# Attention scores by two half-arrays of 64 rows, the zero-padded queries removed, TensorE's attention steps written out

## What is computed

```python
q = split_heads(layernorm(x) @ Wq.T + bq) * 16 ** -0.5      # bq in block 1 only
k, v = split_heads(ctx @ Wk.T + bk), split_heads(ctx @ Wv.T + bv)
logits = einsum('bhqd,bhkd->bhqk', q, k) + bias             # block 1: a mask instead
x = x + einsum('bhqk,bhkd->bhqd', softmax(logits), v).reshape(...) @ Wo.T + bo
```

## Time and profile before

| | us |
|---|---|
| median of 3 runs | 956.08 |
| lowest, highest run | 948.71, 956.51 |
| the profiled execution | 949.21 |
| its span, first to last instruction | 947.2 |
| TensorE busy in the span | 776.4 (82%) |
| VectorE busy | 498.9 (53%) |
| GpSimd busy | 422.4 (45%) |
| ScalarE busy | 293.5 (31%) |

### The profile page before, as it was taken

One profiled execution on the slowest core, in us unless ns is written; L12 is line 12 of the kernel. 1 busy time (PEld: TensorE's weight loads), 2 busy tenths in 40 slices (PEclk: granted clock), 3 DMA queues, 4 the chain that ended last, 5 costly groups with the idle time before them and its releaser, 6 DMA issues. The chain is left out here.

```text
span 947.2 us, 16638 instructions
## 1 busy us (share of the span) xinstructions
PE 776.4 (82%) x4409; PEld 619.4 (65%) x4411; DVE 498.9 (53%) x1644; ACT 293.5 (31%) x804; POOL 422.4 (45%) x463
## 2 busy tenths in 40 slices
PE   4799999687994499999985588889497059999995
PEld 3688887344662367777763477667385059999994
DVE  2788886543331465555543699999472113333331
ACT  1455554011221144444432244444241012212220
POOL 1343342033767344554543776667452133443431
PEclk8999998598998599999998699999795579999998
DMA  7333333401200144444463223334556456555540
GB/s 204 132 128 106 98 116 104 113 18 13 25 8 0 33 127 135 141 142 135 138 125 102 70 76 111 112 111 134 67 67 84 84 180 202 175 183 196 189 164 1
DMA packets 62007, 103.05 MB, mean 109 GB/s; under 512 B 22313, under 2 KB 43273, under 8 KB 60556
## 3 DMA queue, kind: packets, MB, share of 16 engines
q1 hardware_dynamic: 48076, 73.08, 27.3%
q0 software_dynamic: 13600, 27.33, 11.5%
q10 hardware_dynamic: 288, 2.10, 0.6%
HBM read 82.77 MB, written 22.44 MB: 111 GB/s over the span
## 5 line engine op out<-in xcount | busy, mean ns | idle before, releaser
L601 POOL DMA_INDIRECT U<-normed,idx x95 | 91.1, 959 | 97.8 <-DVE idx L1123 79.7
L586 POOL TENSOR_TENSOR U<-U,mx 128x1232 f32<-128x1232 f32 x32 | 72.3, 2258 | 102.1 <-DVE mx L1212 101.8
L1050 PE MATMUL bank<-R,U 128*128 x380 | 104.2, 397 | 6.4 <-issue 3.8
L1095 PE MATMUL bank<-X,R 128*128 128x128 f32 x736 | 87.2, 277 | 0.0
L1095 PEld LDWEIGHTS bank<-X,R 128*128 128x128 f32 x736 | 85.5, 195 | 0.1
L1108 PE MATMUL bank<-R,X 128*128 x368 | 83.1, 379 | 0.0
L1050 PEld LDWEIGHTS bank<-R,U 128*128 128x128 f32 x380 | 65.3, 192 | 21.4 <-issue 12.8
L579 POOL DMA_INDIRECT U<-expert_out,slot_cur x64 | 64.5, 1008 | 22.4 <-issue 14.7
L1108 PEld LDWEIGHTS bank<-R,X 128*128 128x128 f32 x368 | 68.2, 190 | 8.4
L518 POOL DMA_INDIRECT table<-tok_cur,slot_cur x64 | 61.8, 965 | 26.5 <-issue 13.7
L985 PE MATMUL bank<-R,xT 128*128 128x512 f32 x128 | 64.4, 629 | 7.3 <-issue 6.8
(11 more groups left out here) (185 smaller groups left out, 1607.1 us busy)
## 6 DMA issues: line engine op xcount, KB each, us to landing
R<-in_w SPq DMA_DIRECT2D x31, 1024.0 KB, 8.1
R<-in_gu SPq DMA_DIRECT2D x8, 1024.0 KB, 5.6
expert_out<-U SPq DMA_DIRECT2D x48, 128.0 KB
expert_out<-xr SPq DMA_DIRECT2D x47, 128.0 KB, 2.4
normed<-xr SPq DMA_DIRECT2D x32, 128.0 KB, 1.7
R<-in_down SPq DMA_DIRECT2D x8, 512.0 KB, 3.7
x<-X SPq DMA_DIRECT2D x16, 128.0 KB, 2.6
X<-in_x ACTq DMA_DIRECT2D x1, 1536.0 KB, 7.5
```

Source lines behind the costliest of these rows:

```text
L586: pool.tensor_tensor(s3, s3, mx[u][:, :].unsqueeze(2).to_broadcast([P, H, S2]), ALU.subtract).then_inc(T["sub"], 1)
L601: pool.indirect_dma_start(xg0[u], None, xn_d[0], bass.IndirectOffsetOnAxis(idx[u][:, :], 0)).then_inc(EX[0]["gath"][u], 16)
L1050: mm = pe.matmul(bank[2 + u][:, 0:2 * F0], xgT0[u][:, c, :], gu_w[:, c, bass.ds(e, 1), :].rearrange("p a n -> p (a n)"), start=(c == 0), s ...
L1095: mm = pe.matmul(bank[1 + 2 * v + f // 4][:, (f % 4) * P:(f % 4 + 1) * P], w1_of[v][:, c, f * P:(f + 1) * P], xgT1[v][:, c, :], start=(c = ...
```

## The change

ScalarE copies q once, whole, into `qT` of 128 rows and two blocks: one activation for both halves in layer 0, one per block (two) in layer 1. The memset, the semaphore and the wait for the zeros go. Each of the four score products takes 64 rows of `qT` and the same 64 rows of `kbd`, rows 0 to 63 and 64 to 127 in turn, into the same four banks as before. TensorE's attention program no longer has a loop: steps -5 to 18 are all written out, with constants in waits and addresses; the other engines keep theirs.

```diff
-        qz = sb("qz", [P, KC, 2, P])
+        qT = sb("qT", [P, KC, P])
@@ gpsimd
-            pool.memset(qz[:, :, :, :], 0.0).then_inc(q_zero, 1)
@@ scalar
-                        for half in range(2):
-                            r = slice(64 * half, 64 * half + 64)
-                            if l == 0:
-                                ins = act.activation(qz[r, :, half, :],
-                                                     bank[4][r, 0:D].rearrange("p (c n) -> p c n", c=KC),
-                                                     ACT.Copy, scale=DH ** -0.5)
-                            else:
-                                for c in range(KC):
-                                    ins = act.activation(qz[r, c, half, :], bank[4][r, c * P:(c + 1) * P],
-                                                         ACT.Identity, bias=bq4[r, c:c + 1], scale=DH ** -0.5)
+                        if l == 0:
+                            ins = act.activation(qT[:, :, :].rearrange("p c n -> p (c n)"), bank[4][:, 0:D],
+                                                 ACT.Copy, scale=DH ** -0.5)
+                        else:
+                            for c in range(KC):
+                                ins = act.activation(qT[:, c, :], bank[4][:, c * P:(c + 1) * P],
+                                                     ACT.Identity, bias=bq4[:, c:c + 1], scale=DH ** -0.5)
                         ins.then_inc(T["q"], 1)
...
-            act.wait_ge(q_zero, 1)
@@ tensor
-                                           vbd[l][0:rows, bass.ds(batch(t, 0) * PC + c, 1), 0:cols].rearrange(
-                                               "p a n -> p (a n)"),
+                                           vbd[l][0:rows, batch(t, 0) * PC + c, 0:cols],
...
                             c, half = g // 2, g % 2
-                            mm = pe.matmul(bank[g][:, 0:HG * S2], qz[:, c, half, :],
-                                           kbd[l][:, bass.ds(batch(t, 2) * KC + c, 1)].rearrange(
-                                               "p a h k -> p (a h k)"), start=True, stop=True)
+                            r = slice(64 * half, 64 * half + 64)
+                            mm = pe.matmul(bank[g][:, 0:HG * S2], qT[r, c, :],
+                                           kbd[l][r, batch(t, 2) * KC + c].rearrange("p h k -> p (h k)"),
+                                           start=True, stop=True)
...
-                attention_steps(pe, step)
+                for t in range(-5, NT + 3):
+                    place[0] = t % 2
+                    step(t)
```

More of the change, by code:

```diff
@@ L291, in build @@
         bo_in = sem("bo_in")
-        q_zero = sem("q_zero")
         waited_apart = sem("waited_apart")
```

## The result

The kernel after takes 945.58 us (median of 20 runs, 939.16 to 960.18) against 952.15 of the kernel before (20 runs, 942.83 to 963.84, mixed with them). The ratio is 0.9934, with a 95% interval of 0.9911 to 0.9956: 6.3 us less, between 4.2 and 8.5. 944 was predicted, from a gain of 8.75 us, just outside that interval. A ratio here leaves out the executions that took over 1.5% longer than the fastest of the same kernel, three of these 20 and up to four of six in the experiments, where the median of all executions then stands beside it. The profiled execution took 943.61 us (span 941.7) where before's took 949.21.

A forecast was written before the change was run, and what follows sets the result against it. TensorE was taken to bound layer 0's tiles, a VectorE and GpSimd ring layer 1's. Terms of 4.2 + 0.3 + 1.9 + 1.35 + 1.0 = 8.75 us gave 940.5 from the profile, 947.3 from the median; forecast 944, range 934 to 957.

The forecast's parts named there:

- Pairing: Score products of each tile: 0.81 of 2.16 us saved by overlap, net 0.5 us per tile after 0.3 for switching.
- the switches: TensorE entering and leaving the half array around the score products: 0.23 + 0.06 = 0.3 us per tile.
- What is late next: Layer 0's steady tiles: L866 waits for L1240, so the period shrinks only 0.35 us to 8.08; twelve periods give 4.2 us.
- Layer 0's filling: First tile of layer 0: copy of q saves 0.39 us, cold scores 1.5, together 1.9 us.
- Layer 1's filling: Second layer's start: q and scores 2.1 us earlier, but GpSimd's gathers let only 1.35 us pass on.
- Layer 1's steady tiles: Second layer's tiles: a VectorE and GpSimd ring sets the pace and TensorE waits for it, so gain 0.
- this rival: Anything else, such as TensorE's clock falling because it streams less; chance 5%.
- Layer 1's emptying: Last two tiles with scores in the second layer: TensorE on the path again, 0.5 us each, 1.0 us.
- Edits costed at nothing: Memset of qz and its wait, shorter copy of q in steady tiles, TensorE's loop written out: taken as 0.
- The sum: Whole kernel: 4.2 + 0.3 + 1.9 + 1.35 + 1.0 = 8.75 us gained.
- The late gather: Second layer, VectorE standing 10.34 us for one tile's gathers: gone gives 931 to 937, doubled 951 to 957; chance 15%.

The follow-up runs named there:

- the order 0, 2, 1, 3: Kernel after with the four score products issued in that order, two on rows 0 to 63 first; ratio to before 0.9985 (0.9943 to 1.0027).
- the second profile: Kernel after, unchanged, run and profiled once more; ratio to before 0.992 (0.9889 to 0.9951).
- written-out kernel: Kernel before with only TensorE's attention program written out; zero-padded q and products over 128 rows stay; ratio to before 1.0004 (0.996 to 1.0048).
- the fillers: Kernel after plus unread identity products where TensorE waits, in both fillings and layer 1's tiles; ratio to before 0.9888 (0.9842 to 0.9933).
- layer 1 twice: Kernel after with each of layer 1's four score products issued twice into the same bank; ratio to before 0.9878 (0.9838 to 0.9918).
- the logits apart: Kernel after with the router's logits (and layer 1's ranks) in bank 6 instead of bank 4; ratio to before 0.9857 (0.9777 to 0.9938).
- one half: Kernel after with all four score products on rows 0 to 63, some scores wrong; ratio to before 1.0042 (1.0008 to 1.0076).
- full rows in layer 1: Kernel after with layer 1's score products over all 128 rows, its scores wrong; ratio to before 0.997 (0.9935 to 1.0004).

## Why the prediction was nearly right, step by step

The pairing and the wait behind it are right in mechanism. The sum came out near for another reason as well: TensorE's clock took back part of the gain in two places, which I had put at nothing, and one tile at the end gave more than I had counted. The range, 934 to 957, was so wide that it would have held without any gain.

**Pairing, mis-sized and without consequence.** I took records in program order, 0.81 us saved, and less 0.3 for the switches. Pairing is complete, 1.04 saved (four records at 0.26), and the switches cost 0.26. Both sizes end at L860's wait for lg, as I had written, so the error cost nothing in the steady tiles. The Trainium skill, TensorEngine Tiling (Array Packing), section Key Properties, says that a change of tiling mode drains TensorE; the trace agrees, and the price is those 0.26 us. The Trainium skill, TensorE: Matmul & The Clock Gate, Part 3, has products on different rows start some 4 ns apart, in program order at their start and at their end. Here they start 6 to 7 ns apart, 12 to 14 in the order 0, 2, 1, 3, and the starts did not keep that order between the halves: there the measurement decides. Of the ends the trace has the completion signals, and these agree with the page.

**What is late next, right.** 8.08 us predicted, 8.02 measured twice; the wait is where I put it, with VectorE idle 0.89 (0.85 predicted) and the four additions in 1.62 (1.65). Third to fourteenth reciprocal: 92.7 us before, 88.2 after. That is 4.5 us for eleven of the periods, against 3.85 by my term. The twelfth, just before them, got longer instead, from 8.43 to 9.89 and in the second profile 9.03, with TensorE at 1.2 GHz from 43.8 to 50.7 us (45.0 to 48.4).

**Layer 0's filling, wrong.** 1.9 us predicted. GpSimd's first subtraction does start 2.2 us earlier (26.34, 28.57), and the first reciprocal starts 0.8 earlier, at 36.29. The 2.2 us were there, so the copy and the scores are right. What failed is that I let the gain pass from L586 to the first reciprocal unchanged. Behind L586 come the exponentials and then TensorE's own work, the transposes up to the product with the values. Before (timeline, 17 to 37.5 us):

```profile
32.13 0.66 PE L817 MATMUL bank<-ident,U 128*128 128x128 f32 x4 [2.69 <-ACT U L704]
...
34.75 2.32 PE L893 MATMUL bank<-R,U 128*128 128x51 f32 x20
...
37.10 0.26 DVE L1298 RECIPROCAL rs<-bank 128x16 f32<-128x16 f32 x1 [1.57 <-PE bank L893]
```

and after (timeline, 14 to 60 us):

```profile
29.90 1.11 PE L811 MATMUL bank<-ident,U 128*128 128x128 f32 x4 [1.77 <-ACT U L699]
...
33.93 2.32 PE L887 MATMUL bank<-R,U 128*128 128x51 f32 x20
...
36.29 0.26 DVE L1294 RECIPROCAL rs<-bank 128x16 f32<-128x16 f32 x1 [3.00 <-PE bank L887]
```

The transposes start 2.2 us earlier and the reciprocal 0.8. Between them lie 4.97 us before and 6.39 after (7.11 in the second profile), and VectorE waits for TensorE 3.00 us instead of 1.57. The granted clock was back at 2.4 GHz at 24.4 us before, and only at 33.6 after. The written-out kernel of the padded q also had 3.4 us of low clock in this piece, and 6.26 us for it, so the price is the clock's; that the pairing made the clock stay low longer here isn't shown.

**Layer 1's filling, right in mechanism.** From the start of layer 1's attention to the first subtraction it is 23.9 us before, 22.4 and 22.6 in the two profiles after: 1.4 us (1.35 predicted). GpSimd's last gather ends at 533.48 and the subtraction starts at 533.50, as I had argued. Of the 1.4 us 0.9 and 1.2 reach the first reciprocal.

**Layer 1's steady tiles, wrong.** I wrote 0, and named the granted clock of 0.95 at 80% busy as evidence against a fall of the clock. That was the wrong reading: a clock of 1.00 in these tiles shows that their present work is enough, not that less would be. The loss was 3.6 us in one profile and 0.4 in the other. I had given this rival, with others, 5%.

**Layer 1's emptying, right in sign and too small.** 1.0 us predicted. From the thirteenth to the sixteenth reciprocal it took 29.96 us before, 23.0 and 25.1 after. That is 6.9 and 4.9 us, and most of it is one tile, which nothing in my argument foresaw and which I count as luck: before, the clock fell at 710.4 and the last period took 12.65 us; after, it fell at 716.3, when that tile was done (7.25). In the written-out kernel it fell at 712.6, with 12.7 us for the tile. In the eight profiles whose clock held until the last tile was done, that period is 7.25 or 7.26. In the order 0, 2, 1, 3 the clock fell early in it and it took 11.7. In that of the fillers it is 11.8, although the clock fell only towards its end: VectorE stood 6.0 us there for something that no row names, and the cause isn't found. Nor is it settled why the full clock between the last two low stretches lasted only 20 us in before, in the written-out kernel and in the order 0, 2, 1, 3, and 24 to 34 in the others.

**Edits costed at nothing, right** where they were tried: the written-out program leaves layer 0's period at 8.43. The shorter copy of q and the memset were not tried apart.

**The sum.** 8.75 us predicted, 6.3 measured (4.2 to 8.5). By the two profiles the attention stages alone gained 8.9 and 11.6 us. To the sixteenth reciprocal of layer 0 it is 3.8 and 5.1, where I had 6.4; from the start of layer 1's attention to its sixteenth reciprocal 5.0 and 6.5, where I had 2.35. So the sum is near because the last tile of layer 1 made good what the clock took in layer 0's filling and in layer 1's tiles. There is one profile of before to compare with, and the stages between, which no edit touches, differ by more than all this from one execution to the next. Why the medians show 6.3 and not 8.9 or 11.6 isn't settled. The late gather stayed as it was: 24.1 us from the twelfth to the thirteenth reciprocal before, 23.3 and 23.4 after, 20.2 to 23.8 in the rest.

## What to carry to other kernels

Work over half the rows of TensorE could be paired in full here, at some 0.26 us for going in and out, and the gain is real only as far as the next wait behind it allows: look for that wait first, and move it in the same edit (here the logits' bank, 0.3 us more per tile). Work taken from TensorE in a stage where it was not the bound can make that stage slower through its clock; look at the granted clock of every stage, after as well as before. Giving TensorE work back where it waits restored the clock in the tiles here, and what it is worth for the whole has to be measured each time. A low clock costs where TensorE is on the path, as from the first exponentials to the first reciprocal, so ask of each low stretch what waits for TensorE in it.

## What the runs showed of the hardware

Float32 products on different halves of the rows start 6 to 14 ns apart, record by record, even if the program puts two products of the same half first; their completion signals then still come in program order (1.33 and 1.37 us after the burst's start, instead of 0.81 and 1.33). A product over 64 rows takes as long as one over 128 (0.26 us per record of 308 columns at 2.4 GHz). With the same eight records per tile, TensorE's clock held 2.4 GHz over 128 rows and fell to 1.2 for 27.3 us in twelve tiles over 64. Paired halves fell in every profile of a kernel without added work in layer 1 (17 to 41 us); with the products issued twice they did not, or once for 6.8 us. One profile of each kernel but one stands behind these figures; the mean clock of the timed runs agrees with them: 0.89 to 0.92 in before and in the written-out kernel, 0.87 to 0.89 in after and in the one with the logits apart, 0.88 to 0.905 on one half and 0.89 to 0.905 with full rows in layer 1, 0.89 to 0.91 with layer 1 twice (one outlier left out), 0.91 to 0.92 with the fillers.
